# Reordering the shared expert around the routing step of a gated cross-attention block, with a wider ring for routed rows and two loads moved to GpSimd

## What is computed

```python
x = x + tanh(g_xattn) * xattn(layernorm(x), ctx, mask, Wq, Wk, Wv, Wo)
x = x + tanh(g_ffn) * ffn(layernorm(x), ...)

# inside ffn, after its self-attention: h is [800, 512]
h = rms(x, w_ln2)
probs = softmax(h @ w_router)
top_w, top_i = top_k(probs, 2)
routed = sum over the two chosen experts of top_w * (silu(h @ w_gate_e) * (h @ w_up_e)) @ w_down_e
sh = silu(h @ w_sh_gate) * (h @ w_sh_up) @ w_sh_down * sigmoid(h @ w_sh_eg)
x = x + routed + sh
```

## Time and profile before

| what | us |
|---|---|
| median of 3 runs | 976.92 |
| the three runs | 974.06, 979.06, 976.92 |
| the profiled execution, its time | 981.73 |
| its span in the trace | 979.9 |

### The profile page before, as it was taken

One profiled execution on the slowest core, in us unless ns is written; L12 is line 12 of the kernel. 1 busy time (PEld: TensorE's weight loads), 2 busy tenths in 40 slices (PEclk: granted clock), 3 DMA queues, 4 the chain that ended last, 5 costly groups with the idle time before them and its releaser, 6 DMA issues.

```text
span 979.9 us, 16173 instructions
## 1 busy us (share of the span) xinstructions
PE 901.8 (92%) x5713; PEld 836.0 (85%) x5713; DVE 654.4 (67%) x1466; ACT 565.6 (58%) x1455; POOL 397.8 (41%) x373
## 2 busy tenths in 40 slices
PE   5999999999999999999879888799857989999996
PEld 4889999999989999999857766598857989999896
DVE  3557776742637777742696956666855788898863
ACT  3656666644546666653344756545335767777661
POOL 3432222345432322336654421044462555565431
PEclk9999999999999999999997989699978999999999
DMA  5766710025530000006322111022486989999875
GB/s 150 210 231 187 208 52 2 11 73 148 160 101 16 1 2 1 12 28 175 92 79 65 44 46 42 12 87 86 131 275 197 280 270 318 286 302 306 252 195 149
DMA packets 118040, 129.41 MB, mean 132 GB/s; under 512 B 13188, under 2 KB 81228, under 8 KB 117360
## 3 DMA queue, kind: packets, MB, share of 16 engines
q1 hardware_dynamic: 98862, 104.74, 34.6%
q0 software_dynamic: 5120, 10.22, 5.2%
q10 hardware_dynamic: 13978, 13.41, 4.7%
HBM read 110.81 MB, written 26.19 MB: 140 GB/s over the span
## 4 chain that ended last, share of the span: by engine, by line
PE 61%; DVE 16%; DMA 9%; issue 5%; ACT 5%; POOL 3%; ACTq 0%; POOLq 0%; DVEq 0%; SPq 0%
PE bank L2012 55%; PE bank L2141 4%; DMA s_sum<-yo,target 2%; DMA eraw<-in_L_ffn_w_down_e_dram 2%; DVE we L1339 2%; ACT we L905 1%; DVE PQ L1520 1%; POOL s_rows L1942 1%; DMA s_rows<-HR,idx 1%; DVE HR L1336 1%; DVE PQ L1518 1%; DVE sm L1543 1%; DMA eraw<-in_L_ffn_w_gate_e_dram 1%; DMA sums<-s_sum 1%; DVE wf L1339 1%
## 5 line engine op out<-in xcount | busy, mean ns | idle before, releaser
L1902 POOL TENSOR_SCALAR SC<-SC,mx,anyv 100x361 f32<-100x361 f32 x128 | 81.4, 646 | 211.2 <-DVE mx L1451 200.9
L1873 POOL TENSOR_TENSOR wf<-raw,wf 128x512 fp32r<-128x512 f32 x54 | 72.6, 1350 | 138.2 <-ACT wf L891 138.2
L1885 POOL TENSOR_TENSOR we<-eraw,we 128x704 fp32r<-128x704 f32 x40 | 74.1, 1852 | 99.5 <-ACT we L905 99.4
L1873 POOL TENSOR_TENSOR wx<-raw,wx 128x512 fp32r<-128x512 f32 x64 | 83.2, 1311 | 76.0 <-ACT wx L891 75.8
L905 ACT ACTIVATE we<-eraw 128x704 fp32r<-128x704 f32 (+2 forms) x140 | 96.8, 718 | 28.1 <-DMA eraw<-in_L_ffn_w_down_e_dram 13.1
L1339 DVE TENSOR_TENSOR we<-eraw,we 128x704 fp32r<-128x704 f32 (+2 forms) x100 | 92.8, 944 | 22.6 <-ACT we L905 22.4
L2012 PE MATMUL bank<-H2h,wf 128*128 128x400 f32 x352 | 99.7, 351 | 0.0
L1021 ACT ACTIVATE SC<-SC,mx 100x361 f32<-100x361 f32 x128 | 75.4, 593 | 29.3 <-DVE mx L1447 28.9
L2012 PE MATMUL bank<-XTh,wx 128*128 128x400 f32 x256 | 72.3, 356 | 3.7 <-POOL wx L1873 2.3
L1339 DVE TENSOR_TENSOR Kl<-bank,Kh 128x362 fp32r<-128x362 f32 x64 | 34.1, 535 | 60.3 <-ACT Kh L979 60.3
L1339 DVE TENSOR_TENSOR QOl<-bank,QOh 128x200 fp32r<-128x200 f32 (+1 forms) x96 | 41.5, 432 | 46.2 <-ACT QOh L934 36.2
(11 more groups left out here) (259 smaller groups left out, 2784.0 us busy)
## 6 DMA issues: line engine op xcount, KB each, us to landing
raw<-s_unit SPq DMA_DIRECT2D x60, 256.0 KB, 3.7
eraw<-in_L_ffn_w_gate_e_dram SPq DMA_DIRECT2D x40, 352.0 KB, 4.1
eraw<-in_L_ffn_w_up_e_dram SPq DMA_DIRECT2D x40, 352.0 KB, 5.4
eraw<-in_L_ffn_w_down_e_dram SPq DMA_DIRECT2D x40, 256.0 KB, 5.8
raw<-in_L_xattn_Wq_dram SPq DMA_DIRECT2D x32, 256.0 KB, 3.1
raw<-in_L_xattn_Wo_dram SPq DMA_DIRECT2D x32, 256.0 KB, 2.9
s_rows<-Z SPq DMA_DIRECT2D x6, 800.0 KB
XB<-s_rows ACTq DMA_DIRECT2D x18, 256.0 KB, 5.6
```

The costliest lines, as they stand in the source:

```text
L1873: eng.tensor_tensor(w[:, 1, :, :], raw[plan.raw[stream, u] % 4][:, :, :], f32(w[:, 0, :, :]), ALU.subtract).then_inc(sem("pool_w"), 1)
L1885: eng.tensor_tensor(w[0:rows, 1, 0:n], eraw[u % 6][0:rows, 0:n], f32(w[0:rows, 0, 0:n]), ALU.subtract).then_inc(sem("pool_e"), 1)
L1902: eng.tensor_scalar(sc, sc, m[:, 3, h:h + 1], anyv[:, b:b + 1], ALU.mult, ALU.mult).then_inc(sem("pool_p"), 1)
```

## The change

1. `steps_ffn`: beside the first 10 groups of the epilogue go two units each, so all 20 gates and ups of half 0. Beside `esoft`, `etop1`, `etop2` go 2, 1 and 2 downs. After `rank`, `rows(0)` has nothing beside it and `rows(1)` to `rows(7)` have one down each. The four first `fetch_e` no longer stand behind `rows(4)` to `rows(7)`, but behind the first four units of half 1. Two more units follow ahead of `xt 0`, so six in all. `steps_routed` gets 17 groups, 16 gates and ups and one group of three downs, and 9 downs are left.
2. `xload 0` and `xload 1` stand ahead of those six units, and POOL issues them, on its own queue, with `metas` between them. SP and ACT no longer do.
3. Rows have six tiles: three more, HX, lie in the space of H2h of half 0. `rows(3)` to `rows(5)` wait for the last up of half 0, `rows(6)` and `rows(7)` for the scatters of `rows(0)` and `rows(1)`.
4. Semaphores are merged: `dma_wr` into `dma_c2` (waits for 64 in place of 32), `act_pe` and `act_sg` into `act_soft`.

```diff
-    for _ in range(9):
+    for _ in range(10):
         yield from take(ep, 1)
-        yield from take(s0, 1)
-    s0 += down_groups(0)
-    for n in (2, 1, 1, 3):
+        yield from take(s0, 2)
+    s0 = down_groups(0)
+    for n in (2, 1, 2):
         yield from take(ep, 1)
         yield from take(s0, n)
     yield ("rank",)
     for b in range(B):
         yield ("rows", b)
-        yield from take(s0, 1)
-        if b >= B - AHEAD["e"]:
-            yield ("fetch_e",)
-    s1 = s0 + [g for j in range(NJ) for g in up_groups(j, 1)] + down_groups(1)
-    yield from take(s1, 4)
+        if b:
+            yield from take(s0, 1)
     yield ("xload", 0)
     yield ("xload", 1)
+    s1, last = [g for j in range(NJ) for g in up_groups(j, 1)], down_groups(1)
+    s1 += [take(last, 3)] + last
+    for _ in range(AHEAD["e"]):
+        yield from take(s1, 1)
+        yield ("fetch_e",)
+    yield from take(s1, 2)
     yield ("xt", 0)
     yield ("xload", 2)
-    yield from steps_routed(s1, len(s1) - 10)
+    yield from steps_routed(s1, len(s1) - len(last))
...
+    HX = Region(nc, spare0, spare0 + 4 * KD * HT).ring("HX", 3, [T, XW])
+    row_tile = [HR[(2 * B + b) % 3] for b in range(3)] + HX + [HR[(2 * B + b) % 3] for b in range(2)]
...
-    row_slot = [(2 * B + b) % 3 for b in range(B)]
+    row_slot = [b % 6 for b in range(B)]
...
         def rows(b):
-            n = 2 * B + b
+            t = row_tile[b]
             if b < 3:
                 dve.wait_ge(sem("pe_eh"), B - 3 + b + 1)
+            elif b < 6:
+                dve.wait_ge(sem("pe_up"), NJ)
             else:
-                dve.wait_ge(sem(f"dma_sc{row_slot[b]}"), rows_stored[b - 3])
+                dve.wait_ge(sem(f"dma_sc{row_slot[b]}"), rows_stored[b - 6])
...
+        def x_load_block(i):
+            if i >= 2:
+                return
+            for b in range(B - 6, B):
+                pool.wait_ge(sem(f"dma_sc{row_slot[b]}"), rows_stored[b])
+            pool.wait_ge(sem("pe_up"), NJ)
+            eng.dma_start(XB[i % 2][:, :], s_rows[i * 128:(i + 1) * 128, 0:D]).then_inc(sem(f"dma_xs{i}"), 16)
+            if i == 0:
+                src = s_rows[0:NB * 128, D:XW].rearrange("(n p) c -> p n c", p=128)
+                eng.dma_start(metas[:, :, :], src).then_inc(sem("dma_meta"), 16)
```

More of the change, by code:

```diff
@@ L793, in load_part @@
             eng.dma_start(dst, src).then_inc(sem(f"dma_er{u % 6}"), 16)
[L795 to L801, removed]
         def store(b):
@@ L856, in sync_program @@
                 asked["e"] += 1
-            elif name == "xload":
-                x_load_block(*a)
             elif name == "srow" and a[0] == 1:
@@ L1078, in ffn_constants @@
             act.wait_ge(sem("pool_const"), CONST["router"])
-            eng.dma_start(WR[:, :, 0:NE], kpn(w_router)).then_inc(sem("dma_wr"), 16)
-            eng.dma_start(WR[:, :, NE:NE + 1], kpn(sh_eg), allow_slow_non_contiguous=True).then_inc(sem("dma_wr"), 16)
+            eng.dma_start(WR[:, :, 0:NE], kpn(w_router)).then_inc(sem("dma_c2"), 16)
+            eng.dma_start(WR[:, :, NE:NE + 1], kpn(sh_eg), allow_slow_non_contiguous=True).then_inc(sem("dma_c2"), 16)
         def qk(h, n):
@@ L1142, in esoft @@
             act.wait_ge(sem("dve_pr"), h + 1)
-            eng.activation(pr[:, :, :], pr[:, :, :], ACT.Exp).then_inc(sem("act_pe"), 1)
-            eng.activation(L[:, :, NE:NE + 1], L[:, :, NE:NE + 1], ACT.Tanh, scale=0.5).then_inc(sem("act_sg"), 1)
+            eng.activation(pr[:, :, :], pr[:, :, :], ACT.Exp).then_inc(sem("act_soft"), 1)
+            eng.activation(L[:, :, NE:NE + 1], L[:, :, NE:NE + 1], ACT.Tanh, scale=0.5).then_inc(sem("act_soft"), 1)
         def gate(j, h):
@@ L1183, in x_load_block @@
         def x_load_block(i):
[L1184 to L1188, removed]
             if i >= 2:
@@ L1529, in v_row @@
                 dve.wait_ge(sem("pe_fv"), HB * k + i + 1)
-                dve.wait_ge(sem("dma_c2"), 32)
+                dve.wait_ge(sem("dma_c2"), 64)
                 eng.tensor_tensor(V[0][:, i, :], banks[i][0:T, :], bvb[:, :], ALU.add).then_inc(sem("dve_v"), 1)
@@ L1621, in etop1 @@
         def etop1(h):
-            dve.wait_ge(sem("act_pe"), h + 1)
+            dve.wait_ge(sem("act_soft"), 2 * h + 1)
             chained(eng.tensor_reduce(r1[:, 0, :], pr[:, :, :], AX, ALU.add))
@@ L1677, in rows @@
         def rows(b):
-            n = 2 * B + b
+            t = row_tile[b]
             if b < 3:
                 dve.wait_ge(sem("pe_eh"), B - 3 + b + 1)
+            elif b < 6:
+                dve.wait_ge(sem("pe_up"), NJ)
             else:
-                dve.wait_ge(sem(f"dma_sc{row_slot[b]}"), rows_stored[b - 3])
+                dve.wait_ge(sem(f"dma_sc{row_slot[b]}"), rows_stored[b - 6])
             dve.wait_ge(sem("dve_route"), ROUTE["sg", 1])
             dve.wait_ge(sem("pool_const"), CONST["orders"])
-            eng.tensor_copy(HR[n % 3][:, D:D + NE], share[:, b, :]).then_inc(sem("dve_rows"), 1)
-            eng.tensor_copy(HR[n % 3][:, D + NE:XW], token[:, b:b + 1]).then_inc(sem("dve_rows"), 1)
-            stt(HR[n % 3][:, 0:D], Z[:, b, :], rz[:, b:b + 1], ln2b[:, :], ALU.mult, ALU.mult).then_inc(sem("dve_rows"), 1)
+            eng.tensor_copy(t[:, D:D + NE], share[:, b, :]).then_inc(sem("dve_rows"), 1)
+            eng.tensor_copy(t[:, D + NE:XW], token[:, b:b + 1]).then_inc(sem("dve_rows"), 1)
+            stt(t[:, 0:D], Z[:, b, :], rz[:, b:b + 1], ln2b[:, :], ALU.mult, ALU.mult).then_inc(sem("dve_rows"), 1)
         def meta():
@@ L1924, in router_split @@
         def router_split():
-            pool.wait_ge(sem("dma_wr"), 32)
+            pool.wait_ge(sem("dma_c2"), 64)
             eng.tensor_copy(WRh[:, :, :], WR[:, :, :]).then_inc(sem("pool_const"), 1)
@@ L2000, in pool_program @@
                 rows(*a)
+            elif name == "xload":
+                x_load_block(*a)
             elif name == "give":
@@ L2403, in x_block @@
             bank = free_bank(("xt", i))
-            pe.wait_ge(sem(f"dma_xb{i % 2}"), 16 * (i // 2 + 1))
+            pe.wait_ge(sem(f"dma_xb{i % 2}" if i >= 2 else f"dma_xs{i}"), 16 * max(i // 2, 1))
             v = XB[i % 2].rearrange("s (p k) -> s k p", k=KD)
```

4 lines of the change are left out of this document (2 added, 2 removed).

## The result

| kernel | median us | lowest to highest | runs |
|---|---|---|---|
| before | 979.02 | 974.06 to 981.66 | 10 |
| after | 985.71 | 978.04 to 989.32 | 10 |

The ratio is 1.0063, with a 95% interval from 1.0040 to 1.0087: the change costs 0.6%, just more than a measurement can tell from no change. The forecast was 978 with a range of 969 to 987. The time lies in the range, near its upper end. The likeliest case, within 0.5% of before, did not come about by the median, though the interval begins inside it. The profiled execution of after ran 985.63 with a span of 983.8.

A forecast was written before the change was run, and what follows sets the result against it. PE, busy 92%, was taken to set the time wherever it does not wait. 758.7 + 177.5 + 44.9 = 981.1 against a span of 979.9, +1.2, gave 978 from the 976.9 median; own range 974 to 982, whole range 969 to 987.

The forecast's parts named there:

- PE up to rank: Epilogue and softmax steps: four more gates and ups and five more downs move rank from 692.1 to 710.7.
- Rank to the first scatter: Routing step: DVE begins 0.6 us after PE and needs 6.6 more, so the first scatter goes out at 717.9.
- Scatters: Routing step: the 16 scatters take 25 us, between 20.6 and 30.8, the last landing at 745.4.
- PE's own work: Behind rank: 7 downs and 6 units end at 738.4, so PE pauses once, for longer, in place of twice.
- The crossing of queues: Last landing to first routed matmul: part 6 waits for POOL's part 0, delaying ACT's copy of block 0; 10.3 + M.
- M: POOL's issue of metas, 2,560 runs of 36 bytes, between the block loads: taken as 3 us, from 0.84 to 10.8.
- rival C: GpSimd's loads are slow: M goes toward 10.8, +7.8 us, time 986; chance 0.12.
- A: Rival: the crossing does not bind, first routed matmul near 752.7, 6.0 us earlier, time 972; chance 0.20.
- B: Rival: short scatters, 20.6 us in place of 25, and M = 0.84, time 971.5; chance 0.12.
- The routed stage: First routed matmul to POOL's last part: 195.2 falls to 177.5 us; PE alone 174.2, transfers 169.0; range 174 to 185.7.
- Rival D: Transfers become the routed stage's bound: share stays 0.91, stage 185.7, +8.2 us, time 986; chance 0.14.
- The tail: After POOL's last part: stays 44.9 us, set by the scatter-adds.

The follow-up runs named there:

- e2: The changed kernel with both block loads moved behind the four units and their fetch_e: 985.52 us, ratio 1.0054.
- e4: The changed kernel with eight eraw slots in place of six, SP two parts further ahead: 972.06 us, ratio 0.9930.
- e6: The kernel before with only the six row tiles and the merged semaphores, order and loads as before: 978.2 us, ratio 0.9985.
- e7: e6 with eight eraw slots and SP's reach bounded as in e9: 965.63 us, ratio 0.9851.
- e9: e4 with SP kept at six parts until the first block is asked for: 970.19 us, ratio 0.9900.
- e11: e6 with five shared-expert unit steps taken ahead of the transposes of block 0, still six slots: 984.84 us, ratio 1.0050.
- e3: The changed kernel with 8 groups beside the routed blocks in place of 17, the other units after the stage: 994.1 us, ratio 1.0151.
- e1: The changed kernel with the first two block loads on SP and metas on ACT again: 991.0 us, ratio 1.0119.
- e10: e7 with five shared-expert unit steps taken ahead of the transposes of block 0: 963.25 us, ratio 0.9836.

## Why the prediction held, and where it did not

**PE up to rank.** Predicted 18.6 later, measured 17.9 by the means of thirteen kernels. In the one profile of after it is 14.1. The term was right within 0.7 us, the single execution was not typical.

**Rank to the first scatter.** 7.2 predicted, 6.9 measured (706.24 to 713.09).

**Scatters.** 25 us predicted, 23.7 measured (713.09 to 735.29 + 1.48). The instructions alone took 19.1. The last landed at 739.9.

**PE's own work** ended at 733.6, so 27.4 behind rank, as predicted (738.4 - 710.7 = 27.7).

**The crossing of queues** went as written: SP's part 6 at the end of POOL's first part, ACT idle for the unit behind it, the copy of block 0 late. From the landing to the first routed matmul it took 10.7 us. The sum gave 10.3 + M.

**M** was taken as 3 and is 1.36. So rival C is refuted. The two XB issues took 0.62 and 0.56. The direction fits what the Trainium skill says ("DMA: Bandwidth & Descriptors", "Anatomy of one DMA") of many descriptors before an extra cost shows: 20 times the runs of a block load took 2.2 to 2.4 times as long to issue. The Trainium skill's other rule, from "SBUF — State Buffer" (the "DVE blocks DMA" trap), is not tested in after, since DVE did nothing at all from 740.0 to 743.3. In e2 DVE was busy 2.10 of the 2.5 us of these three issues, and they took 0.63, 1.36 and 0.57 us all the same. The 3.1 us each that the prediction allowed for did not appear.

**Rivals A and B.** Rank to first routed matmul was predicted as 48.0 and took 44.3: 0.3 from the first scatter, 0.7 from the scatters to the landing, 2.6 behind it. A, in which the copy of block 0 doesn't wait, is refuted in after by ACT's 9.58 us. e2 shows it realised, for nothing. B came about in part (M, and 1.3 us of scatters).

**The routed stage is the step that failed.** The text took 177.5 from "both limits, 3 us apart from it", with a lower limit of 169.0 for the transfers at 304 GB/s. Measured are 187.1, 9.6 more, and outside the bounds of 174 to 185.7. The limit wasn't PE's work and wasn't the DMA engines' either, but the loop through six slots. 24 units in it took 195 us, 14 units took 187, 19 took 196. With eight slots the 14 take 171 to 173 us. That is near PE's sum, 174.2, and the transfers run at 302 GB/s, near the 304: the two limits were roughly those of a kernel with eight slots. But 304 was no ceiling, since the middle 60 us of e4 ran at 318. The 12.9 us by which the stage exceeds PE's sum are of two kinds. PE idles 14.7 us in it, where the sum kept the 6.5 of before, and its matmuls take 172.4 us, where the sum has 188.7 - 21 = 167.7. The clause "with six slots to smooth it" was the error. The earlier trace rows gave no reason to trust six slots, and ACT's waits for loads of parts, 22.3 us in the stage of before, were there to be read. By the prediction's own sign, a stage that stays above 183 us, it is wrong, although the total lies in its range.

**Rival D** is right in its number (share 0.91, stage above 183) and wrong in its reason. It read the share as a saturated engine. e4 runs the same bytes at a share of 0.97.

**The tail** took 46.2, not 44.9, +1.3, within what it spreads over in kernels that don't touch it (43.0 to 47.3).

**Merged semaphores** cost nothing that shows: e6 has them, together with the six tiles, and is at 0.9985.

The total came near by luck, because errors of both signs met: 3.7 us too many between rank and the first routed matmul, and 4.5 more because rank itself stood early in this execution, against 9.6 too few in the stage and 1.3 in the tail. The upper end of the range, 987, stood for C or D, and of these only D's number came true. The forecast's own range, 974 to 982, does not hold the time. On medians the forecast is 7.7 us low, 2.1 of which is that the median of before rose from 976.92 to 979.02 with more runs.

**What stays open.** Whether the new order costs or is neutral once the slots are eight: the intervals of e7 and e9 overlap. Why PE idles more in the six-slot stage when five units are taken out of it, and why ten units give back 0.8 us each there and the next eight 1.7. A kernel with fewer bytes for the downs and the same six slots wasn't run.

## What to carry to other kernels

Before moving work out of a stage, ask whether PE bounds that stage: follow the chain within it. If loads of a ring of buffers stand in it, the work beside them is partly free, and moved elsewhere most of its time counts. How much of it is free has to be measured: here from more than all (e11) to a fifth (e3) of a unit's time. Two more buffers alone gave 1.2%. The new order of steps gave nothing, and where it was alone (e1 against e6) it cost about 1.3%. A DMA share near 0.9 over a long stage doesn't say that the transfers are at their limit. And where a wait is undone by reordering queues, look at what the load then runs beside: the block load took 6.2 us in place of 3.3.

## What the runs showed of the hardware

- A DMA share of 0.91 with 277 GB/s was no ceiling: with two more buffers the same transfers ran at 0.97 and 302 GB/s over 171 us, and at 318 GB/s in the middle 60 us, where the share reads 1.03. So the share isn't a fraction with a top at 1.
- A unit of 256 KB lands 3.2 us after its issue by the median over the whole of after. In the routed stage, while other loads are under way, a unit takes 6.7 us and a part of 256 KB 6.3 by the median, and 7.6 in the piece of the chain shown.
- GpSimd issued a plain DMA of 2,560 runs of 36 bytes in 1.36 us, and one of 128 rows in 0.56 to 0.62.
- In PE's 17.1 us pause the granted clock was 0.57, near the lower of its two levels, and over the 187 us behind it 0.97. It was 1.00 before the pause. In e11 and e10 the same 1007 matmuls took 183.84 us at 0.95 and 176.34 us at 0.99.
